# Attention with a relation bias on one core: key logits kept in SBUF, one ring of query tiles, and the bounds stored and fetched between the copies of a unit

## The reference

```
q, k, v  = x @ Wq.T + bq, x @ Wk.T + bk, x @ Wv.T + bv      # 16 heads of width 16
logits   = li[i] + lj[j] + rel_b                            # three relation logits per pair (i, j)
probs    = softmax(logits over the three)
bias     = sum_k probs[i, j, k] * logical_bias[h, k]
scores   = q.k / sqrt(16) + sigmoid(x @ gate_W.T + gate_b)[i, h] * bias
out      = softmax(scores over j) @ v @ Wo.T + bo
```

## Time and profile before

| | us |
|---|---|
| median of 3 runs | 5028.67 |
| lowest and highest | 5019.67, 5031.66 |
| the profiled execution | 5015.02 |
| its span | 5013.2 |
| PE, PE weight loads, DVE, ACT, POOL busy in the span | 3750.1, 2787.7, 3755.9, 3323.6, 2024.0 |

### The profile page before, as it was taken

How to read it: one execution, slowest core, us unless ns; L and a number is a source line. 1 busy time by engine, 2 the same in 40 slices (tenths; PEclk the granted TensorE clock), 3 DMA queues, 4 the chain that set the end, 5 groups by cost and what they waited for, 6 DMA issues and landing times. The chain is left out here.

```text
span 5013.2 us, 248173 instructions
## 1 busy us (share of the span) xinstructions
PE 3750.1 (75%) x106896; PEld 2787.7 (56%) x106896; DVE 3755.9 (75%) x6310; ACT 3323.6 (66%) x3946; POOL 2024.0 (40%) x1816
## 2 busy tenths in 40 slices
PE   7457777777777777777777778777777776289992
PEld 4225555555555555555555555555555555257772
DVE  4498887888888888888888788888888843167773
ACT  2128777777777777877787777877777883034440
POOL 0114444444444444444444444444444442433335
PEclk8669999999999999999999899999999998589996
DMA  6213333333333333333333333333333335244443
GB/s 107 67 38 95 97 98 95 95 97 98 97 94 93 96 96 97 100 95 94 98 97 95 94 95 95 100 98 98 95 97 98 96 103 190 77 145 146 155 138 113
DMA packets 405084, 510.32 MB, mean 102 GB/s; under 512 B 109296, under 2 KB 343152, under 8 KB 400016
## 3 DMA queue, kind: packets, MB, share of 16 engines
q1 hardware_dynamic: 394800, 476.50, 31.2%
q0 software_dynamic: 6144, 16.79, 1.1%
q10 hardware_dynamic: 3040, 0.98, 0.1%
HBM read 237.99 MB, written 46.40 MB: 57 GB/s over the span
## 5 line engine op out<-in xcount | busy, mean ns | idle before, releaser
L732 DVE TENSOR_REDUCE b_mxp<-b_mx 128x1 f32<-128x512 f32 x4096 | 2579.7, 680 | 531.3 <-PE b_mx L848 509.4
L704 ACT ACTIVATE b_pr<-b_sc 128x1024 f32<-128x1024 f32 x2048 | 1982.4, 1020 | 893.0 <-PE b_sc L829 874.1
L871 PE MATMUL b_acc<-b_pr,vp 128*32 128x128 f32 x32768 | 1207.3, 288 | 25.2 <-issue 23.2
L848 PE MATMUL b_mx<-kst,b_qx 64*128 64x512 f16 x4096 | 849.8, 410 | 415.5 <-DVE b_mxp L732 399.1
L815 PE MATMUL b_sc<-b_cm,b_rst 64*128 64x64 f16 x32768 | 789.9, 196 | 494.8 <-DMA b_rst<-b_rhi 343.0
L627 POOL TENSOR_TENSOR b_ex<-b_ex 128x512 f32<-128x512 f32 x512 | 676.2, 1321 | 990.0 <-ACT b_ex L682 987.3
L815 PEld LDWEIGHTS b_sc<-b_cm,b_rst 64*128 64x128 f16 x32768 | 679.7, 98 | 690.0 <-issue 437.7
L871 PEld LDWEIGHTS b_acc<-b_pr,vp 128*32 128x32 f32 x32768 | 892.9, 115 | 304.9 <-issue 288.8
L724 DVE TENSOR_SCALAR b_dl<-b_dj,b_const 128x512 f32<-128x512 f32 x1024 | 693.5, 679 | 193.7 <-DMA b_dj<-key_logits 191.9
L637 POOL CAST b_rhi<-b_ex 128x512 f16<-128x512 f32 x512 | 325.6, 636 | 1089.4 <-ACT b_ex L691 977.8
L829 PE MATMUL b_sc<-b_qm,kst 64*128 64x64 f16 x32768 | 716.4, 195 | 37.1 <-issue 34.4
(11 more groups left out here) (144 smaller groups left out, 1627.8 us busy)
## 6 DMA issues: line engine op xcount, KB each, us to landing
b_dj<-key_logits SPq DMA_DIRECT2D x256, 512.0 KB
b_rst<-b_rhi SPq DMA_DIRECT2D x1024, 128.0 KB
b_rst<-b_rlo SPq DMA_DIRECT2D x512, 128.0 KB
c_w1r<-in_L_ffn_W_dram SPq DMA_DIRECT2D x23, 1024.0 KB, 4.8
c_w2r<-in_L_ffn_W_dram SPq DMA_DIRECT2D x23, 1024.0 KB, 4.8
expert_tokens<-c_zeros SPq DMA_DIRECT2D x23, 512.0 KB, 6.8
c_xb<-expert_tokens SPq DMA_DIRECT2D x23, 512.0 KB
expert_results<-c_y SPq DMA_DIRECT2D x23, 512.0 KB, 2.9
```

The source lines that it names most:

```text
L704: nc.scalar.activation(pr[:, jt % 2, half, :], sc[:, half].rearrange("p a b -> p (a b)"), ACT.Exp).then_inc(s["p_ready"], 1)
L732: nc.vector.tensor_reduce(mxp[:, head, part:part + 1], mx[:, (bank + ab) % MX_RING, :], AX.X, ALU.max).then_inc(s["mx_used"], 1)
L848: pe.matmul(mx[:, (bank + ab) % MX_RING, :], qx[rows, par, pair, :], kst[rows, pair, j0:j0 + 512], start=True, stop=True).then_inc(s["mx_r ...
L871: ins = pe.matmul(acc[32 * (h % 4):32 * (h % 4) + 32, h // 4, :], vp[:, jt, VW * h:VW * h + 32], pr[:, jt % 2, h % 2].rearrange("p (a h i) ...
```

## The change

Four things change:

- The key logits have a buffer for each of the 8 units (`b_dj`, 32 KB a partition in place of 8 KB). They are loaded once, units 0 and 1 on the semaphore `dj_in0`, the others on `dj_in1`. In the chunks there is no key-logit load and no wait for one, on SP or on DVE.
- One ring of four query tiles `qt` replaces `qm` and `qx`. A tile is loaded once, two transfers of 128 KB, after unit 2, for the chunk after next, and serves the maxima and later the products. For this the rows of `kst` take the order high, high, low, low, where they had high, low, high, low. SP's wait of L600 for `c_made` goes.
- In unit 6 the bounds are stored right after the first step of the copies (with the wait for L742 ahead of the store), and fetched after the third (with the wait for the store). Steps two, three and four stand behind these.
- The loop has 3 turns of 8 chunks, and 8 chunks follow it, so that the slot of the ring is known in each chunk's code.

```diff
-UNROLL, LOOPS = 10, 3
+UNROLL, LOOPS = 8, 3
+QR = 4
@@ project_inputs
-                            for row, part in ((0, 0), (16, 1), (32, 0), (48, 1)):
+                            for row, part in ((0, 0), (16, 0), (32, 1), (48, 1)):
@@ attend
-        dj = sb("dj", [P, 2, 2, JU])
+        dj = sb("dj", [P, UNITS, 2, JU])
-        qm = sb("qm", [P, 2, PAIRS, P], F16)
-        qx = sb("qx", [P, 2, PAIRS, P], F16)
+        qt = sb("qt", [P, QR, PAIRS, P], F16)
...
+        def sp_q(sp, x, par, slot4):
             for ab in range(2):
+                sp.dma_start(qt[64 * ab:64 * ab + 64, slot4].rearrange("r q t -> r (q t)"),
+                             q_dram[bass.ds(x, 1), ab].rearrange("o a r q t -> o (a r) (q t)").broadcast_to(
+                                 [2, 2 * HD, PAIRS * P])).then_inc(s[f"q_in{par}"], 16)
@@ sync, ahead of the chunks
+            for u in range(2, UNITS):
+                sp_dj(sp, u)
...
-            for u in range(2, 4):
-                sp.wait_ge(s["d_ready"], 4 * (u - 1))
-                sp_dj(sp, u)
@@ sync, chunk
-                    if u == M_UNIT and not last:
-                        sp_m_out(sp, c + 1)
-                        sp_m_in(sp, c + 1, 1 - par)
-                    if u + 4 < UNITS or not last:
-                        sp.wait_ge(s["d_ready"], 32 * c + 4 * u + 12)
-                        waited(sp)
-                        sp_dj(sp, (u + 4) % UNITS)
+                        if u == M_UNIT and step == 0 and not last:
+                            sp_m_out(sp, c + 1)
+                        if u == M_UNIT and step == 2 and not last:
+                            sp_m_in(sp, c + 1, 1 - par)
                     if u == 1:
                         sp_att(sp, c)
-                    if u == 2 and not last:
-                        sp_q(sp, c + 1, 1 - par, qm, "q_in")
-                    if u == 3 and more:
-                        sp.wait_ge(s["c_made"], 2 * c + 2)
-                        waited(sp)
-                        sp_q(sp, c + 2, par, qx, f"qx_in{par}")
+                    if u == 2 and more:
+                        sp_q(sp, c + 2, par, (slot4 + 2) % QR)
@@ vector
-            if side == 0 and n == 0:
-                dve.wait_ge(s[f"dj_in{u % 2}"], 16 * (UNITS // 2 * x + u // 2 + 1))
...
+            dve.wait_ge(s["dj_in0"], 32)
...
+            dve.wait_ge(s["dj_in1"], 16 * (UNITS - 2))
```

More of the change, by code:

```diff
@@ L83, in in_chunks @@
         for n in range(UNROLL):
-            chunk(turn * UNROLL + n, n % 2, turn * (UNROLL // 2) + n // 2 + 1, False)
+            chunk(turn * UNROLL + n, n % 2, turn * (UNROLL // 2) + n // 2 + 1, False, n % QR)
     for c in range(LOOPS * UNROLL, NT):
-        chunk(c, c % 2, c // 2 + 1, c == NT - 1)
+        chunk(c, c % 2, c // 2 + 1, c == NT - 1, c % QR)
 def bank_owner(jobs, n, ring=8):
@@ L491, in waited @@
             sp.sem_inc(s["sp_waited"], 1)
-        def parts_twice(x, ab, part):
-            return q_dram[bass.ds(x, 1), ab, part].rearrange("o r q t -> o r (q t)").broadcast_to([2, HD, PAIRS * P])
-        def sp_q(sp, x, par, t, arrived):
+        def sp_q(sp, x, par, slot4):
             for ab in range(2):
[L500 to L503, removed]
+                sp.dma_start(qt[64 * ab:64 * ab + 64, slot4].rearrange("r q t -> r (q t)"),
+                             q_dram[bass.ds(x, 1), ab].rearrange("o a r q t -> o (a r) (q t)").broadcast_to(
+                                 [2, 2 * HD, PAIRS * P])).then_inc(s[f"q_in{par}"], 16)
         def sp_dj(sp, u):
-            sp.dma_start(dj[:, u % 2].rearrange("p n j -> p (n j)"),
-                         dj_dram[u].rearrange("(k n) j -> k (n j)", k=2).unsqueeze(1).broadcast_to([2, IS, 2 * JU])).then_inc(s[f"dj_in{u % 2}"], 16)
+            sp.dma_start(dj[:, u].rearrange("p n j -> p (n j)"),
+                         dj_dram[u].rearrange("(k n) j -> k (n j)", k=2).unsqueeze(1).broadcast_to([2, IS, 2 * JU])).then_inc(s[f"dj_in{min(u // 2, 1)}"], 16)
         def sp_consts(sp, x, par):
@@ L557, in _ @@
         def _(sp):
-            sp_q(sp, 0, 0, qx, "qx_in0")
+            sp_q(sp, 0, 0, 0)
             sp.wait_ge(s["cval_zeroed"], 1)
@@ L575, in _, with chunk @@
             sp_m_in(sp, 0, 0)
-            def chunk(c, par, nth, last):
+            def chunk(c, par, nth, last, slot4):
                 more = not last and not (isinstance(c, int) and c + 2 >= NT)
@@ L817, in pe_relation, with pe_products @@
             return ins
-        def pe_products(pe, c, par, jt):
-            if jt == 0:
-                pe.wait_ge(s["q_in"], 64 * c + 64)
+        def pe_products(pe, c, slot4, jt):
             for turn in range(2):
@@ L829, in pe_products @@
                         ins = pe.matmul(sc[:, ab, side, pair * IS:pair * IS + IS], kst[rows, pair, jt * P:jt * P + P],
-                                        qm[rows, par, pair, side * IS:side * IS + IS], start=False,
+                                        qt[rows, slot4, pair, side * IS:side * IS + IS], start=False,
                                         stop=(pair == PAIRS - 1), skip_group_check=True)
@@ L833, in pe_products, with pe_scores, pe_pair, pe_step_pair @@
                             ins.then_inc(s["scores_ready"], 1)
-        def pe_scores(pe, c, par, jt):
+        def pe_scores(pe, c, par, slot4, jt):
             pe_relation(pe, c, par, jt, 0)
             pe_relation(pe, c, par, jt, 1).then_inc(s["relation_done"], 1)
-            pe_products(pe, c, par, jt)
-        def pe_pair(pe, x, par, nth, n, bank):
+            pe_products(pe, c, slot4, jt)
+        def pe_pair(pe, x, par, nth, slot4, n, bank):
             pair, j0 = n // MXU, n % MXU * 512
             if n == 0:
-                pe.wait_ge(s[f"qx_in{par}"], 64 * nth)
+                pe.wait_ge(s[f"q_in{par}"], 32 * nth)
             for ab in range(2):
                 rows = slice(64 * ab, 64 * ab + 64)
-                pe.matmul(mx[:, (bank + ab) % MX_RING, :], qx[rows, par, pair, :], kst[rows, pair, j0:j0 + 512],
+                pe.matmul(mx[:, (bank + ab) % MX_RING, :], qt[rows, slot4, pair, :], kst[rows, pair, j0:j0 + 512],
                           start=True, stop=True).then_inc(s["mx_ready"], 1)
-        def pe_step_pair(pe, c, par, nth, jt, slot, last, more):
+        def pe_step_pair(pe, c, par, nth, slot4, jt, slot, last, more):
             n = 2 * jt + slot + AHEAD
@@ L860, in pe_step_pair @@
             if n < PAIRN and not last:
-                pe_pair(pe, c + 1, 1 - par, nth + par, n, step_bank(jt, slot))
+                pe_pair(pe, c + 1, 1 - par, nth + par, (slot4 + 1) % QR, n, step_bank(jt, slot))
             elif n >= PAIRN and more:
-                pe_pair(pe, c + 2, par, nth + 1, n - PAIRN, step_bank(jt, slot))
+                pe_pair(pe, c + 2, par, nth + 1, (slot4 + 2) % QR, n - PAIRN, step_bank(jt, slot))
         def pe_pv(pe, c, jt):
@@ L890, in _, with chunk @@
                         pe.wait_ge(s["mx_used"], 2 * PAIRN * x + 2 * n - 1)
-                    pe_pair(pe, x, x, 1, n, 2 * PAIRN * x + 2 * n)
+                    pe_pair(pe, x, x, 1, x, n, 2 * PAIRN * x + 2 * n)
             pe.wait_ge(s["ones_made"], 1)
-            pe_scores(pe, 0, 0, 0)
-            def chunk(c, par, nth, last):
+            pe_scores(pe, 0, 0, 0, 0)
+            def chunk(c, par, nth, last, slot4):
                 more = not last and not (isinstance(c, int) and c + 2 >= NT)
@@ L898, in chunk @@
                     if jt < NT - 1:
-                        pe_scores(pe, c, par, jt + 1)
+                        pe_scores(pe, c, par, slot4, jt + 1)
                     elif not last:
-                        pe_scores(pe, c + 1, 1 - par, 0)
-                    pe_step_pair(pe, c, par, nth, jt, 0, last, more)
+                        pe_scores(pe, c + 1, 1 - par, (slot4 + 1) % QR, 0)
+                    pe_step_pair(pe, c, par, nth, slot4, jt, 0, last, more)
                     pe_pv(pe, c, jt)
-                    pe_step_pair(pe, c, par, nth, jt, 1, last, more)
+                    pe_step_pair(pe, c, par, nth, slot4, jt, 1, last, more)
                     if jt == OUT_AT:
```

7 lines of the change are left out of this document (3 added, 4 removed).

## The result

| | before | after |
|---|---|---|
| median of the runs, us | 5024.17 (4 runs) | 4540.84 (4 runs, 4525.04 to 4553.5) |
| profiled execution, us | 5015.02 | 4540.25 |
| its span, us | 5013.2 | 4538.5 |
| DMA engines' traffic, MB | 510.32 | 371.66 |

The ratio after / before is 0.9038, with a 95% interval from 0.9004 to 0.9071: the changed kernel is 9.6% faster. Predicted were 4578 us and a range from 4480 to 4750.

A forecast was written before the change was run, and what follows sets the result against it. DVE's idle time, 21 us a chunk, was taken as the bound, passed on from PE's late copies behind two-engine key-logit loads. Savings of 451 us take the profiled 5015.0 to 4564; plus 13.7 for the median, 4578, range 4480 to 4750.

The forecast's parts named there:

- Key logits resident: In each chunk, removing the 512 KB loads and DVE's waits for them shortens the chunk from 121.3 to 105.7 us.
- misses of the bounds: In unit 6, SP's added wait for the bounds sometimes makes the last copies late: 0.5 us a chunk.
- One query load: After unit 2, the single load of 256 KB comes some 4 us ahead of unit 4's copies; priced at nothing.
- free chain: Unit 6 with free engines: store to fetch 1.47 us, fetch 1.51, step four 1.2, landing 1.9; 6.1 in all, within 7.4.
- price with loaded engines: Unit 6 with engines as loaded before: store to fetch 4.94 us, 13.9 in all, so copies 6.5 us too late.
- rival B: Unit 6: the bounds' wait replaces the stalls, up to 6.5 us late; 4677 us (half) or 4773 (all), chance 0.15.
- C: Copies land late by themselves, both long stalls stay and unit 7 gets a new one; slower, 5149 us, chance 0.04.
- Loop of 8: Chunk loop: two jumps back as before, at no cost.
- Ahead of the chunks: Before chunk 0, DVE waits for both first units of key logits: 6.8 us slower, once.
- The sum: Whole run: 15.1 us for 30 chunks, plus 5 for the last two, minus 6.8, gives 451 us saved.
- A: Ahead of unit 4, the query load on two engines keeps a 5.9 us stall: 4750 us, chance 0.13.
- What would show it: Profile signs: right if chunks take 104 to 108 us and DVE is 93% busy; wrong if copies land 5 us late.

## Why the prediction was right

- *What bounds the kernel: DVE's idle time, handed on from PE's wait for copies, caused by the two-engine load.* Right, and shown by the four runs on the load: few engines cost 300 us and more, with or without a reader; the same bytes on sixteen engines don't hold the copies.
- *Key logits resident, a chunk of 105.7 us.* Measured 105.6 with all changes. The way to it, DVE's work divided by its share in an undisturbed stretch, held, and two small errors cancelled: the share was 0.953 and not 0.945, the work 100.7 us a chunk (1906.87 us in 2000 / 105.6 = 18.9 chunks) and not 99.9. The 0.5 us a chunk for misses of the bounds were too much: PE waits 4.3 us for copies in 19 chunks, 0.2 each, though all of it stands ahead of unit 7, where the misses had been expected.
- *One query load at no cost.* Right: the issues take 1.44 us and end 3 us ahead of the next step, and none of PE's four waits for copies stands behind them.
- *The bounds.* The free chain was right: 1.92 us from store to fetch (1.47 foretold, 2.32 the longest of all chunks), and the copies in time in 15 chunks of 19. In the chunk shown they are there 2.5 us after their issue at the latest; in the three with waits of 1.2 to 1.6 us the last one took some 3 us, where 1.9 had been foretold. The price with loaded engines, 6.5 us a chunk, was wrong by far: the run that moved only the bounds has stalls of 1.9 us in the mean there, and a small gain in sum. This price was the whole of rival B and a part of C.
- *Loop of 8: "two jumps back as before, no cost".* Right as a difference, though the jumps themselves cost something. DVE's rows of `b_att` put the two chunks with a jump at 128.6 and 128.1 us before, where the others take about 121, and at 115.4 and 115.7 after, where they take about 105. The jump holds what is now the longest wait of DVE between 1000 and 3000 us (7.60).
- *Ahead of the chunks.* 6.8 us foretold. The first bounds come at 320.64 in the changed kernel and at 314.26 before, 6.4 later.
- *The sum.* 4564 foretold for the profiled execution, 4540.25 measured, 24 less. 29 chunks gave 15.7 us each, not 15.1: 17 of the 24 us. Up to the first marked row 4.4 us were gained (430.24 - 425.81), as much as the sum has there (three quarters of a chunk less 6.8). The rest is in the end: from the last marked row to the end of the span it takes 1066.4 us before (5013.2 - 3946.83) and 1051.3 after (4538.5 - 3487.21), 15 less, where the sum has a quarter of a chunk and 5 us, about 9. For the median 13.7 us more had been added, because the profiled execution before was that much below its median; the one after is 0.6 us below its own. So 37 us lie between the forecast of 4578 and 4540.84.
- *Rivals.* A (the query load keeps its stall) didn't come true here, and the resident key logits alone show that two such loads don't stall either; it holds only while key logits are loaded, as the ring alone showed. B (the bounds' wait takes the stalls' place) would need a stall of up to 6.5 us ahead of unit 7; the longest between 1000 and 3000 us is 1.6, and putting the bounds back changes nothing that the runs can tell. C would have needed copies that are slow on their own; they land in 2 to some 3 us as soon as the two-engine load is gone.
- *What would show it.* Every sign for "right" came. One sign for "wrong" came too, and was badly chosen: ACT's waits were to shrink only if DVE's idle time turned to another engine's pace, but ACT's waits for the scores fell from 413.2 us to 186.5 between 1000 and 3000. They had to, as ACT has the same work in a shorter chunk: it is busy for 89.6% of the stretch (1792.46 us), about the 90% foretold, and DVE with 95.3% still more.

## What to carry to other kernels

When copies or loads wait longer to be issued than they take, look at the DMA share while one transfer is alone in flight: here a share of 0.13 to 0.14, near 1/8, meant two engines, and what comes behind that transfer pays for it, whoever reads its data. Cut such a transfer so that its outer dimension is the rows, before thinking about keeping its data resident: here that alone gave 7.8%, where residence gave 9.4%. To price the removal of stalls, divide the work of the busiest engine by its busy share in a stretch without them. Parts of a change that remove the same stall don't add up, and a new stall ahead of an old wait is partly paid by that wait.

## What the runs showed of the hardware that I had not expected

- Code that runs in a loop of 8 chunks costs PE more idle time without a semaphore, in all chunks and not at the jumps alone: 43.6 + 29.7 us in 2000 us in the loop (waits of the changed kernel for L801 and L813), of which the two jumps are 14, and 12.3 + 16.0 written out. What the engine lacks in that time no run shows. With 512 KB per unit on sixteen engines beside it, it is 89.1 + 52.0 in the loop. In that run the eight chunks behind the loop had DVE busy for 96.4% (385.63 of 400 us, the row below), the chunks inside for 91.2% (1823.08 of 2000):

```profile
3250.00:3650.00 400.00, 329.79 (x12084) 246.67 (x12084) 385.63 (x625) 357.81 (x423) 202.34 (x188) 1.00 0.41 107
```

- A four-fold issue of query loads held SP for 9.45 us behind one 512 KB transfer that itself had taken 0.56 us to issue, and for 3.06 us without it: the price of a full engine shows on the next transfer's line, not on its own.
